# A twelve-layer perceiver kernel on one core: the experts' token weights spread by DMA through DRAM and applied by GpSimd

## The reference: what is computed

```python
topk_logits, topk_idx = jax.lax.top_k(logits, TOP_K)
topk_w = jax.nn.softmax(topk_logits.astype(jnp.float32), axis=-1).astype(x.dtype)
comb = jnp.zeros((N, E), x.dtype).at[jnp.arange(N)[:, None], topk_idx].add(topk_w)
...
for e in range(E):
    g = xf @ wg[e].T
    u = xf @ wu[e].T
    y = jax.nn.silu(g) * u @ w_down[e].T
    out = out + comb[:, e:e + 1] * y
shared = jax.nn.silu(xf @ sg_gate.T) * (xf @ sg_up.T) @ sg_down.T
```

## Time and profile before

| | |
|---|---|
| median of 3 runs (range) | 3163.27 us (3159.71 to 3168.95) |
| profiled execution: time, span from first to last instruction | 3161.48 us, 3160.1 us |
| mean granted clock of TensorE | 0.897 of full speed |
| busy: PE, DVE, ACT, POOL | 2623.2, 2062.0, 1138.0, 480.7 us |
| L0f | from about 257 to 507 us |
| L2f | from about 1587 to 2256 us |
| L3f | from about 2799 us to the end |

### The profile page before, as it was taken

How to read it: one execution, slowest core, us unless ns; L and a number is a source line. 1 busy time by engine, 2 the same in 40 slices (tenths; PEclk the granted TensorE clock), 3 DMA queues, 4 the chain that set the end, 5 groups by cost and what they waited for, 6 DMA issues and landing times.

```text
span 3160.1 us, 65795 instructions
## 1 busy us (share of the span) xinstructions
PE 2623.2 (83%) x28350; PEld 1803.7 (57%) x28400; DVE 2062.0 (65%) x5468; ACT 1138.0 (36%) x1680; POOL 480.7 (15%) x420
## 2 busy tenths in 40 slices
PE   5787898777888997777888888888888888779999
PEld 3464556665555554444666666666555555556665
DVE  5777887777545567888755555555655446665655
ACT  2343223443433225555322332332344454522222
POOL 3220003443111320000111111111000013320000
PEclk8798999777888998999988888888899988979999
DMA  3000000000000001000000000000100000000000
GB/s 118 7 1 6 1 6 25 15 13 9 2 2 5 1 16 42 12 6 2 9 14 2 2 2 2 2 2 12 45 12 12 2 1 1 1 1 8 7 7 7
DMA packets 17573, 34.70 MB, mean 11 GB/s; under 512 B 5633, under 2 KB 12417, under 8 KB 16897
## 3 DMA queue, kind: packets, MB, share of 16 engines
q1 hardware_dynamic: 17280, 30.48, 3.2%
HBM read 28.38 MB, written 2.10 MB: 10 GB/s over the span
## 4 chain that ended last, share of the span: by engine, by line
PE 36%; DVE 9%; issue 2%; ACT 2%; POOL 1%; DVEq 0%; ACTq 0%
PE psum L792 5%; PE psum L777 4%; PE psum L781 4%; PE psum L1964 3%; DVE c_L3x_top L1515 2%; PE psum L405 2%; PE psum L1983 2%; PE psum L1399 1%; PE psum L1409 1%; PE psum L2277 1%; PE psum L785 1%; PE psum L1990 1%; DVE c_L2f_y L2177 1%; PE psum L2015 1%; PE psum L1422 1%
## 5 line engine op out<-in xcount | busy, mean ns | idle before, releaser
L819 DVE TENSOR_TENSOR c_L3f_h<-c_L3f_h,psum 128x512 f32<-128x512 f32 (+1 forms) x112 | 76.9, 687 | 118.3 <-PE psum L781 118.3
L807 ACT ACTIVATE c_L3f_h<-psum 128x512 f32<-128x512 f32 (+1 forms) x112 | 66.9, 597 | 237.3 <-PE psum L777 237.2
L792 PEld LDWEIGHTS psum<-weights,c_L3f_h 128*128 128x128 f32 (+1 forms) x896 | 116.3, 191 | 34.6 <-issue 29.6
L792 PE MATMUL psum<-weights,c_L3f_h 128*128 128x128 f32 (+1 forms) x896 | 119.3, 276 | 1.5 <-DVE c_L3f_h L823 0.5
L777 PE MATMUL psum<-c_L3f_xT,weights 128*128 128x512 f32 (+1 forms) x224 | 116.9, 604 | 1.6 <-ACT c_L3f_combT L742 1.3
L781 PE MATMUL psum<-c_L3f_xT,weights 128*128 128x512 f32 (+1 forms) x224 | 115.3, 596 | 0.0
L1515 DVE TENSOR_REDUCE c_L3x_top<-psum 128x16 f32<-128x2048 f32 x32 | 73.4, 2292 | 54.1 <-PE psum L1399 54.1
L1727 PE MATMUL psum<-constants_held,c_L2x_p 128*128 128x128 f32 x512 | 81.4, 313 | 29.8 <-ACT c_L2x_p L1760 29.8
L1727 PEld LDWEIGHTS psum<-constants_held,c_L2x_p 128*128 128x128 f32 x512 | 67.6, 162 | 61.4 <-ACT c_L2x_p L1760 53.5
L1964 PE MATMUL psum<-c_L2f_xT,weights 128*128 128x256 f32 x384 | 100.3, 425 | 0.1
L1760 ACT ACTIVATE c_L2x_p<-c_L2x_p 128x1024 f32<-128x1024 f32 x64 | 67.7, 1057 | 83.4 <-DVE c_L2x_p L1795 81.8
(11 more groups left out here) (637 smaller groups left out, 7079.5 us busy)
## 6 DMA issues: line engine op xcount, KB each, us to landing
c_L0x_ctxT<-ctxT SPq DMA_DIRECT2D x8, 384.0 KB, 8.1
c_L1x_ctx<-ctx SPq DMA_DIRECT2D x16, 192.0 KB, 2.4
c_L2x_ctxT<-ctxT SPq DMA_DIRECT2D x8, 384.0 KB, 3.6
c_L3x_ctxT<-ctxT SPq DMA_DIRECT2D x8, 384.0 KB, 3.6
weights<-weights SPq DMA_DIRECT2D x1, 2628.0 KB, 10.2
weights<-weights SPq DMA_DIRECT2D x1, 2345.0 KB, 9.3
out<-x_held SPq DMA_DIRECT2D x8, 256.0 KB, 2.3
weights<-weights SPq DMA_DIRECT2D x1, 1552.0 KB, 11.5
```

Source lines behind the costliest of these rows:

```text
L792: put = t.matmul(psum[:, 0, k * P:(k + 1) * P], m["h"][0:rows, before % 2, k * P:(k + 1) * P], j.weight("down")[0:rows, before * P:(before ...
L807: s.activation(m["h"][0:rows, f % 2, :], j.psum[0:rows, 1, 0:j.tok], ACT.Silu).then_inc(*j.up("silu"))
L819: v.tensor_tensor(h, h, j.psum[0:rows, 2, 0:j.tok], ALU.mult).then_inc(*j.up("gated"))
```

## The change

1. The spread matmuls and their constant matrices go, and so do the split in bf16 parts and DVE's second multiplication.
2. Instead PE transposes the weights in float32 (`pe_combine`), ACT copies them, and SP writes them to a scratch tensor in DRAM (16x512 or 8x512 or 8x256 float32), waits for that, and reads each expert's row back into all its hidden rows of a new tile `spread` with a stride of zero: 16 transfers in a job of L0f (64x512 each), 16 in L3f (128x512 or 64x512), 8 in L2f (64x256). POOL multiplies `h` by `spread`, chunk by chunk; it waits for the transfers quarter by quarter (`pool_mix`).
3. `h` keeps all chunks. The gates and ups no longer wait for the routing: they use three banks in rotation, and the routing and the downs use bank 0. The downs (`c`), the routing on ACT (`b`) and on DVE (`r`) and the spreads on SP (`s`) are programs of their own, so the order can put them elsewhere. All downs wait for POOL, but for those of the shared expert.
4. ORDER is another string throughout, in layers that the change leaves alone too.
5. Some semaphores get other names (`latT` becomes `small`, and so on), with the same waits.

```diff
-def pe_combine(nc, j, n):
-    t, m = nc.tensor, j.m
-    yield
-    t.wait_ge(*j.at("split", 5))
+def pe_combine(nc, j, comb):
+
+    nc.tensor.wait_ge(*j.at("comb", 1))
     for k in range(j.tiles):
-        put = t.matmul(j.psum[0:3 * n, 3, k * P:(k + 1) * P], m["parts"][:, k, 0:3 * n], j.half["ident"], start=True, stop=True)
+        put = nc.tensor.transpose(j.psum[0:comb.shape[2], 0, k * P:(k + 1) * P], comb[:, k, :], j.c["ident"])
     put.then_inc(*j.up("parted"))
 
 
 def act_combine(nc, j, n):
-    yield
     nc.scalar.wait_ge(*j.at("parted", 1))
-    nc.scalar.copy(j.m["combT"][0:3 * n, :], j.psum[0:3 * n, 3, 0:j.tok]).then_inc(*j.up("combT"))
...
-def pe_experts(nc, j, spread, hidden):
+    nc.scalar.copy(j.m["combT"][:], j.psum[0:n, 0, 0:j.tok]).then_inc(*j.up("combT"))
+
+
+def pieces(experts, hidden):
+
+    cuts = sorted({e * hidden for e in range(experts + 1)} | set(range(0, experts * hidden, P)))
+    return [(lo // hidden, lo // P, lo % P, (hi - 1) % P + 1) for lo, hi in zip(cuts, cuts[1:])]
+
+
+def sp_spread(nc, j, experts, hidden):
+
+
+    nc.sync.wait_ge(*j.at("combT", 1))
+    held = j.core.scratch[j.context.number][0:experts, 0:j.tok]
+    nc.sync.dma_start(held, j.m["combT"][:]).then_inc(*j.up("kept", 16))
+    yield
+    nc.sync.wait_ge(*j.at("kept", 16))
+    quarter = experts * hidden // P // 4
+    for e, f, lo, hi in pieces(experts, hidden):
+        nc.sync.dma_start(j.m["spread"][lo:hi, f, :], held[e:e + 1, :].to_broadcast([hi - lo, j.tok])).then_inc(
+            *j.up(f"spread{f // quarter}", 16))
+
+
+def pool_mix(nc, j, experts, hidden):
+    n = experts * hidden // P
+    quarter = n // 4
+    for f in range(n):
+        yield
+        if f % quarter == 0:
+            count = sum(1 for piece in pieces(experts, hidden) if piece[1] // quarter == f // quarter)
+            nc.gpsimd.wait_ge(*j.at(f"spread{f // quarter}", 16 * count))
+        nc.gpsimd.wait_ge(*j.at("gated", f + 1))
+        h = j.m["h"][:, f, :]
+        nc.gpsimd.tensor_tensor(h, h, j.m["spread"][:, f, :], ALU.mult).then_inc(*j.up("mixed"))
+
+
+def pe_gates(nc, j, hidden):
+
     t, m, psum = nc.tensor, j.m, j.psum
...
-            if f == 0:
-                t.wait_ge(*j.at("combT", 1))
-            else:
-                t.wait_ge(*j.at("silu", f))
-            t.matmul(psum[0:rows, 1, 0:j.tok], j.weight("gate")[:, cols], m["xT"][:], start=True, stop=True).then_inc(*j.up("gate"))
-            yield
-            if f > 0:
-                t.wait_ge(*j.at("gated", f))
-            t.matmul(psum[0:rows, 2, 0:j.tok], j.weight("up")[:, cols], m["xT"][:], start=True, stop=True).then_inc(*j.up("upper"))
-            yield
-            if f > 0:
-                t.wait_ge(*j.at("mixed", f))
-            t.matmul(psum[0:rows, 3, 0:j.tok], spread[:, cols], m["combT"][:], start=True, stop=True).then_inc(*j.up("spread"))
+    for f in range(-(-hidden // P)):
+        rows = min(P, hidden - f * P)
+        cols = slice(f * P, f * P + rows)
+        yield
+        if f > 1:
+            t.wait_ge(*j.at("gated", f - 1))
+        t.matmul(psum[0:rows, 1 + 2 * f % 3, 0:j.tok], j.weight("gate")[:, cols], m["xT"][:], start=True, stop=True).then_inc(*j.up("gate"))
...
+            t.wait_ge(*j.at("silu", f))
+        t.matmul(psum[0:rows, 1 + (2 * f + 1) % 3, 0:j.tok], j.weight("up")[:, cols], m["xT"][:], start=True,
+                 stop=True).then_inc(*j.up("inner"))
+
+
+def act_gates(nc, j, hidden):
+    for f in range(-(-hidden // P)):
+        rows = min(P, hidden - f * P)
+        yield
+        nc.scalar.wait_ge(*j.at("gate", f + 1))
+        nc.scalar.activation(j.m["h"][0:rows, f, :], j.psum[0:rows, 1 + 2 * f % 3, 0:j.tok], ACT.Silu).then_inc(*j.up("silu"))
+
+
+def dve_gates(nc, j, hidden):
+    for f in range(-(-hidden // P)):
+        rows = min(P, hidden - f * P)
+        h = j.m["h"][0:rows, f, :]
+        yield
+        nc.vector.wait_ge(*j.at("silu", f + 1))
+        nc.vector.wait_ge(*j.at("inner", f + 1))
+        nc.vector.tensor_tensor(h, h, j.psum[0:rows, 1 + (2 * f + 1) % 3, 0:j.tok], ALU.mult).then_inc(*j.up("gated"))
+
+
+def pe_downs(nc, j, routed, hidden):
     n = -(-hidden // P)
     for f in range(n):
         rows = min(P, hidden - f * P)
         yield
-        s.wait_ge(*j.at("gate", f + 1))
-        if f >= 2:
-            s.wait_ge(*j.at("down", downs + f - 1))
-        s.activation(m["h"][0:rows, f % 2, :], j.psum[0:rows, 1, 0:j.tok], ACT.Silu).then_inc(*j.up("silu"))
-
-
-def dve_experts(nc, j, hidden):
-    v, m = nc.vector, j.m
+        nc.tensor.wait_ge(*(j.at("mixed", f + 1) if f < routed // P else j.at("gated", f + 1)))
+        for k in range(j.tiles):
+            put = nc.tensor.matmul(j.psum[:, 0, k * P:(k + 1) * P], j.m["h"][0:rows, f, k * P:(k + 1) * P],
+                                   j.weight("down")[0:rows, f * P:(f + 1) * P], start=(f == 0 and k == 0), stop=(f == n - 1),
+                                   skip_group_check=True)
...
+def pe_down_L0f(nc, j):
+    yield
+    pe_combine(nc, j, j.m["w"])
+    yield from pe_downs(nc, j, ALL0, ALL0)
...
+def sp_L0f(nc, j):
+    yield
+    yield from sp_spread(nc, j, EXPERTS0, HID0)
+
+
+def pool_L0f(nc, j):
+    yield from pool_mix(nc, j, EXPERTS0, HID0)
 
 
 def dve_L0f(nc, j):
-    v, m, x = nc.vector, j.m, j.x
+    yield from dve_gates(nc, j, ALL0)
+    yield
+    nc.vector.wait_ge(*j.at("down", 1))
+    nc.vector.tensor_tensor(j.x, j.x, tiled(j.psum[:, 0, :], j), ALU.add).then_inc(*j.up("done"))
...
 ORDER = (
-    "dDddDDldLDvVqdppqQDPQaapddapDDgpgpvvldLDAPAPavvvdGAPPGPVVpddAVVVDldpaapapPgpgpqDDLDvvvAPAPVavvvdQGAPPGPVVpddAVVVDldpaapa"
+    "dDddDDldLDvVqdppqQDPQaapddapDDgpgpvvldLDAPAPavvvdGAPPGPVVpddAVVVDldpaapapPgpgpqDDLDvvvAPAPVavvvdGQAPPGPVVpddAVVVDldpaapa"
```

More of the change, by code:

```diff
@@ L2603, with build @@
     pass
-def build(nc, n_seq, weights, constants, halves, x, ctxT, ctx_tok, mask, out, blocks):
+def build(nc, n_seq, weights, constants, halves, x, ctxT, ctx_tok, mask, out, scratch, blocks):
     core = Core()
-    core.nc = nc
+    core.nc, core.scratch = nc, scratch
     core.places, _ = weight_places(weight_table())
```

431 lines of the change are left out of this document (194 added, 237 removed).

## The result

The changed kernel takes 3239.19 us (median of 4 runs, 3233.79 to 3243.15) against 3164.68 us before: a ratio of 1.0235, 95% interval 1.0211 to 1.0259. It is slower by 2.3%, and outside the range that was given.

The account below looks back on a forecast made before the run. The prediction took PE to bound L3f, PE with DVE nearly as close to bound L0f, and dependent chains to pace L2f. L3f −26, L0f −14 and nil elsewhere made −40 us: 3123 us, range 3080 to 3190.

Parts of the forecast that it names:

- L3f, −26: L3f: sum of spread matmuls gone, float32 transposes, earlier gates and a new wait, −26 us; bounds −34 and −14.
- The spread matmuls' −24: L3f: 112 spread matmuls leave PE, which is the bound there: −24 us.
- The new wait, +8: L3f: PE waits at the downs for POOL, taken as 2 us for each of four pairs: +8 us.
- the fuller start: L3f's start: 8 gates and 7 ups, waiting for tokens alone, fill PE's idle time: −12 us.
- L0f, −14: L0f: DVE is the limit no more, PE waits some 3.3 us; a job takes 26.0 instead of 27.8 us: −14.
- rival C: POOL and DVE hold each other: L0f gives nothing, L2f's routing loses 0.5 to 1 a job; 3137 to 3153 us; chance 0.12.
- The rule weighed in the prediction: L0f's routing: DVE instructions with two SBUF inputs contend with POOL's SBUF reads; 6.4 us a job if each multiplication holds once.
- L2f, nil: L2f: fewer spreads and less DVE work set against waits for the DRAM chain: nil; bounds −24 and +40 us.
- rival B: Downs in L0f, L2f, L3f: the round trip through DRAM lies open, 28 exposures; at +3 us, 3207 us; chance 0.26.
- They cancel: L2f: −3 us a pair from spreads and DVE work against +3 a pair from waits, over 8 pairs.
- The rest, nil: Untouched layers and remaining effects: new interleave with the same instructions, POOL's extra work, SP's issuing: nil, bounds ±10 us.
- B's break-even: L0f, L2f, L3f: each us of extra round trip costs 28 us, so the DRAM rival decides from 1.4 us on.

Follow-up runs that it names:

- e9: Kernel before with the change in L0f alone, POOL's product replaced by three fills that take as long without reading SBUF: 3187.49 us, ratio 1.0044.
- e3: Kernel before with the change in L0f alone, its piece of the order string included: 3207.36 us, ratio 1.0105.
- e6: Kernel before with the change in L0f alone, POOL's product replaced by a tiny fill (128x1), transfers and waits kept: 3160.01 us, ratio 0.9985.
- e13: Kernel before with the change in L2f alone, transfers made only in each context's first job, POOL's products kept: 3128.40 us, ratio 0.9849.
- e1: Changed kernel with the old order string in the untouched layers: 3196.14 us, ratio 1.0075 to the kernel before.
- e8: Kernel before with the new order string alone, in the untouched layers: 3208.26 us, ratio 1.0127.

## Why the prediction was wrong

**L3f, −26: right, by errors that cancel, so partly by luck.** Measured −27. The spread matmuls' −24 and the transposes' +2 are −17 in the steady part: 42.0 − 39.9 = 2.1 us a job. The chunk's price without its spread was taken as 2.82 − 0.22 = 2.60, but the downs take 0.97 in a row and not 0.89. The job before, 41.1, was misread too: from the first downs to the last is less than eight jobs. The new wait, +8, is not there: PE has 299.00 of 300 us of work. The chain to POOL's first product was longer than forecast (11.4 us from L731 at 2954.93 to 2966.35, its transfers landing in 4.8 with 256 KB each behind one another, against 2.4 to 2.6), but PE's order held enough to cover it. That leaves some 10 us for the fuller start, where 12 was forecast.

**L0f, −14: wrong by 50 us, and half of it is rival C.** The step that failed is the period of 26.0 us. Its sum for the stretch from L731 to the last downs was right (19.2 us); "DVE ... 16.5, the limit no more" was not. The rule weighed in the prediction decides: DVE's instructions with two tiles in SBUF are held for as long as POOL's take, five in a row in the job shown, 19 to 25 us (e9 against e3), and the addition behind them makes PE's next transposes late. C had priced it to bring L0f back to where it was; in fact L0f is 36 us slower than before, though the stall at the downs, forecast at 3.3 us a job, is 12.5 us in all eight. The other half is not the hold's: e9, which has none, is still 11 us above the kernel before where −14 was forecast, and even e6, with next to no time on POOL, is only 15 below, where PE's sum of 22.6 promised 42. PE's work was added up at full clock, and the clock went down: over 257 to 548 us it is 0.91, before 0.97 from 257 to 508. In e3's stage PE idles some 24 us more than before and is busy 11 more, with 64 spread matmuls fewer. How that half divides between POOL's pace, the transfers and the clock is open. The Trainium skill's page "SBUF — State Buffer", section "Who interferes with whom", says that such an instruction contends with one of GpSimd that reads SBUF and not with one that only writes: both halves agree with e3 and e9 (maxima of 1192 and 1269 ns, and of 176). My chance of 0.12 for it was too low, with the row of a hold in hand and a routing full of such instructions.

**L2f, nil: wrong by 26 us by the stage and 13 by the ratio, on the side of rival B.** B's condition, a longer round trip, did not come true: the chain was well sized (9.5 to 11.9 us forecast, 9.8 from L731 to the end of POOL's last product at 1917.2), and no wait was near 5 us. The step that failed is "They cancel", −24 against +24. Without the transfers the stage is 36 us below the kernel before (e13), so the gain was there and more; the way through DRAM costs 61. PE's wait at the downs was sized a little small (24 us forecast, 36.8 measured in the changed kernel), and the 40 of the 61 us that are no idle time, an estimated 24 of them clock, were put at nothing: the prediction names the clock under B and prices it nowhere.

**The rest, nil: wrong by 42 us, and by no rival.** "ORDER deals the untouched layers in another interleave, with the same instructions; no row prices it" put an unknown at zero with bounds of ±10. e1 and e8 price it at 42 and 39 us; the prediction's last sentence had named the sign for it. Why L2x in particular idles more is only argued: at the change from one pair of jobs to the next the old string sets c0's context matmuls (L1653) ahead of c1's last outputs (L1736), the new one sets both contexts' last projections ahead of either's new job, so that the two pairs no longer overlap. No run changed that seam alone, and L3x's 21 us, all clock, are not explained.

**B's break-even** was stated as 28 us for each us of round trip; in L3f nothing was exposed, so it was 24 at most.

## What to carry to other kernels

Count what a second elementwise engine does to the first before counting what it takes off it: here a product on GpSimd that reads SBUF held the VectorE instructions with two tiles in SBUF that were ready meanwhile, so such work belongs in stages where VectorE has few of them (L3f, −27 us) and not beside a routing chain (L0f, +36). Don't price a wait of PE by its length alone: in L2f the transfers cost 25 us of waits at the downs and 61 us of time, most of the rest in the time that PE is busy with the same matmuls, at a lower clock. And a string of order that changes in layers left alone is a change like any other: run it by itself first.

## What was not expected of the hardware

- The hold also takes DVE's TENSOR_SCALAR from one tile of 128x128 with two values per row: the norm's `xn` in L0f took 606 ns on the mean of 32 in the changed kernel, 340 before; four that lay beside POOL's products (from 404.28 on, in the job shown) took 3.07 us together.
- Transfers with a source of one row, read into 64 or 128 rows, land in 2.6 us for 64 KB and 3.0 for 128 KB, against 2.4 for `ctx` with 192 KB; in L3f, in trains of 16, they take 4.8 us for 256 KB. The Trainium skill's page "DMA: Bandwidth & Descriptors", section "Anatomy of one DMA — SWDGE (gpsimd) path", gives for transfers issued by GpSimd 2.0 us and the bytes at 436 GB/s, by which 128 KB would be an estimated 2.3 us; here SyncE issues them, and the row, 3.0, decides. SP needs 0.62 to 0.64 us to issue one (4.92/8 in L2f, 10.27/16 in L0f), and with two a chunk that is a bound of its own.
- The clock can cost time where idle time doesn't grow: L3x in e8 is 21 us longer at 0.88 instead of 0.96, with 39.7 us of idle PE against 40.7.
